# A quantised feed-forward layer as one instruction block over 512-token blocks, its preparation inside the attention ahead of it, whose weights are requested earlier

## The reference

```python
# third attention (z = layernorm(x), c = context, per sequence)
Sim = (z @ w1)[:, None] + (c @ w2)[None, :] + (z * w3) @ c.T + b
A = softmax(Sim, axis=1);  hq = A @ c
Batt = softmax(Sim.max(axis=1));  zbar = Batt @ z
out = concat(z, hq, z * hq, z * zbar) @ W_qv + b_qv

# third feed-forward: fake-quantised
def act_quant(x, clip):     # one scale for the whole tensor
    s = sigmoid(clip) * max(abs(x)) / 127
    return clip(round(x / s), -128, 127) * s
def weight_quant(w):        # one scale per row
    s = max(abs(w), axis=1) / 127
    return clip(round(w / s), -128, 127) * s
xq = act_quant(layernorm(x), clip_x)            # 2048 x 256
gate, up = xq @ weight_quant(w_gate).T, xq @ weight_quant(w_up).T    # 2048 x 704
h = act_quant(silu(gate) * up, clip_down)
x = x + tanh(g) * (h @ weight_quant(w_down).T)
```

## Time and profile before

| | us |
|---|---|
| median of 3 runs (lowest, highest) | 1708.45 (1704.81, 1709.36) |
| the profiled execution, its own time | 1710.01 |
| its span in the profile | 1708.2 |
| third attention, from its first instruction to the layernorm's | 1267.2 to 1374.5 |
| third feed-forward, to the fourth attention's first instruction | 1374.5 to 1497.1 |

### The profile page before, as it was taken

How to read it: one execution, slowest core, us unless ns; L and a number is a source line. 1 busy time by engine, 2 the same in 40 slices (tenths; PEclk the granted TensorE clock), 3 DMA queues, 4 the chain that set the end, 5 groups by cost and what they waited for, 6 DMA issues and landing times. The chain is left out here.

```text
span 1708.2 us, 31848 instructions
## 1 busy us (share of the span) xinstructions
PE 1391.2 (81%) x10246; PEld 1184.1 (69%) x10246; DVE 1155.5 (68%) x2511; ACT 934.1 (55%) x2046; POOL 756.7 (44%) x797
## 2 busy tenths in 40 slices
PE   2599978999999999879973889999758916463898
PEld 0345565999999999745563889999757803253787
DVE  6457654787888878469965478778543458777554
ACT  4246642777777777457731367777326236364332
POOL 2323102466666676513221078888203910235444
PEclk8799987999999999889995989999889958685999
DMA  4000015356656565130023056667310010011001
GB/s 162 12 1 2 1 42 194 139 196 218 225 197 242 188 232 209 60 105 1 2 87 123 2 168 219 212 226 213 112 35 1 1 54 1 1 32 58 0 13 38
DMA packets 62369, 171.87 MB, mean 101 GB/s; under 512 B 11761, under 2 KB 43249, under 8 KB 53057
## 3 DMA queue, kind: packets, MB, share of 16 engines
q1 hardware_dynamic: 53440, 146.50, 24.8%
q0 software_dynamic: 8832, 24.13, 4.5%
HBM read 152.25 MB, written 18.35 MB: 100 GB/s over the span
## 5 line engine op out<-in xcount | busy, mean ns | idle before, releaser
L1706 POOL TENSOR_TENSOR l0m_e_DL<-l0m_e_DN,l0m_e_DH 128x256 fp32r<-128x256 f32 x184 | 182.0, 995 | 121.2 <-ACT l0m_e_DH L1545 74.6
L1489 PE MATMUL PS<-l0m_e_CH,l0m_e_UH 128*128 128x256 f32 x736 | 210.8, 286 | 2.0 <-DVE l0m_e_CL L1639 2.0
L1489 PE MATMUL PS<-l0m_e_CL,l0m_e_UH 128*128 128x256 f32 x736 | 209.0, 284 | 0.0
L1489 PE MATMUL PS<-l0m_e_CH,l0m_e_UL 128*128 128x256 f32 x736 | 208.9, 284 | 0.0
L1611 DVE TENSOR_TENSOR l0m_e_UL<-l0m_e_U,l0m_e_UH 128x512 fp32r<-128x512 f32 x184 | 148.9, 810 | 12.1 <-ACT l0m_e_UH L1536 12.1
L1489 PEld LDWEIGHTS PS<-l0m_e_CH,l0m_e_UH 128*128 128x128 f32 x736 | 141.9, 193 | 2.2 <-ACT l0m_e_UH L1536 2.2
L1489 PEld LDWEIGHTS PS<-l0m_e_CL,l0m_e_UH 128*128 128x128 f32 x736 | 142.0, 193 | 0.0
L1489 PEld LDWEIGHTS PS<-l0m_e_CH,l0m_e_UL 128*128 128x128 f32 x736 | 142.0, 193 | 0.0
L1623 DVE SCALAR_TENSOR_TENSOR Z<-PS,l0m_e_BU,Z 128x256 f32<-128x256 f32 x184 | 88.7, 482 | 73.3 <-ACT Z L1553 70.9
L1553 ACT ACTIVATE Z<-PS,l0m_e_BU 128x256 f32<-128x256 f32 x184 | 87.7, 476 | 83.1 <-PE PS L1489 83.0
L1536 ACT CAST l0m_e_UH<-l0m_e_U 128x512 fp32r<-128x512 f32 x184 | 113.1, 615 | 0.0
(11 more groups left out here) (531 smaller groups left out, 4519.6 us busy)
## 6 DMA issues: line engine op xcount, KB each, us to landing
l0m_e_U<-in_l_up SPq DMA_DIRECT2D x23, 2048.0 KB
...
```

Of the source, the lines that this page charges most:

```text
L1489: ins = nc.tensor.matmul(hb(f)[:, a * SLOTS:(a + 1) * SLOTS], w[:, f % RING, k, a, :], x[:, j, k, :], start=(p == 0), stop=(p == len(passe ...
L1706: nc.gpsimd.tensor_tensor(DL[:, f % RING, :], DN[:, j, f, :], DH[:, f % RING, :].bitcast(F32), ALU.subtract).then_inc(s_dl, 1)
```

## The change

Three things. The third attention's weights are requested by SP in the second layer's last block, in the middle of `Combine.load`, and layers 2 (feed-forward) and 3 (attention) share one `end_layer`, as do the third feed-forward and the fourth attention. Weight preparation, layernorm and the scale of Z are written into the attention's steps. And the feed-forward is one block.

```diff
+        def l2_load(sp):
+            for tile, array in ((l2["WQ"][:, :, :], I["L2_xattn_W_qv"].rearrange("(k p) n -> p k n", p=P)),
+                                (l2["WC"][:, :, :], I["l2_wsim_cols"]), ...
                 for b in range(B):                      # Combine.load
+                    if b == self.RING:
+                        l2_load(sp)
 # l2_attention, sync: l2_bqv_rows, then the feed-forward's clips, up rows and down rows
 # tensor, between queries(t - 4) and out_rows(t - LAG):
+                            if B + 2 <= t < B + 9:
+                                turn_weights(t - B - 2)      # 6 bf16 transposes; the last: one 128x256 f32 product
 # gpsimd, ahead of the steps, and behind them:
+                        nc.gpsimd.partition_all_reduce(f2["SX"][:, 2:3], f2["ONES"][:, 0:1], P, ...)
                         for t in range(B + GROUP + 4):
 ...
+                        pool.wait_ge(f2["s_largest"], 6)
+                        nc.gpsimd.partition_all_reduce(f2["SX"][:, 2:3], f2["PM"][:, 5:6], P, ...)
 # scalar: exp of the clips at t == 4; copies of the turned weights at t = 18 to 24;
 # deviations at t = 19, 23; normalised rows 0 to 3 and 4 to 7 at t = 20, 21, 8 to 11 at t = 24
 # vector, at the end of each step:
+                        def prepare(t):
+                            if t in (2, 3):        # WR: 128 x 6 x 256, to 128 x 6
+                                wch.step(nc.vector.tensor_reduce(WS[:, 1, halves[t - 2]], WR[:, halves[t - 2], :], ...))
+                            if t == 4:             # WD 128 x 2 x 704, then scale and reciprocal
+                            if 5 <= t < 9:         # three a step
+                                for n in range(3 * (t - 5), 3 * (t - 5) + 3):
+                                    wch.step(nc.vector.tensor_scalar(WR[:, n, :], WR[:, n, :], WS[:, 1, n:n + 1], ROUND, ...))
+                            if t == 9:             # two of 128 x 704
+                            if t in (10, 11, 12):  # clip: 128 x 1536, 1536, 1408
+                            if t in (13, 14, 15):  # to bf16: the same sizes
+                            if t == 16:            # DG
+                            prepare(t)
+                            if t == B + 2: next_scales(0)       # statistics of sequences 0 to 7
+                            if t == B + 3: next_factors(0)
+                            if t == B + 6: next_scales(1)       # 8 to 11
+                            if t == B + 7: next_factors(1)
+                            if t in (B + 6, B + 7):             # largest of Z, four sequences each
+                                next_largest(n, 4 * n, 4 * n + 4)
+                        next_scales(2)                          # behind the last step: 12 to 15
+                        next_largest(2, 8, 12)
+                        next_factors(2)
+                        for b in (12, 13): ...                  # normalised rows on DVE (14, 15 on ACT)
+                        next_largest(3, 12, 14)
+                        next_largest(4, 14, 16)
+                        nc.vector.tensor_reduce(PM[:, 5:6], PM[:, 0:5], AX, ALU.max)
+                        dve.wait_ge(f2["s_all_largest"], 2)
+                        scale_steps(wch, SX, CL[:, 0:1])
 # l2_ffn, scalar, one block:
+                        for u, (n, ch) in enumerate(units):
+                            if ch == 0 and 1 <= n and n + 1 < NBLK:
+                                round_z(n + 1)
+                            silu(u)
+                            if ch == 1 and n + 1 < NBLK:
+                                whole_z(n + 1)
+                            if ch == 4 and n + 1 < NBLK:
+                                copy_z(n + 1)
+                        act.wait_ge(s_hst, 2)
+                        for n in range(NBLK):
+                            for q in range(4):
+                                nc.scalar.activation(part, part, ACT.Identity, scale=SH[...], bias=RND[...])   # round, in place
+                                if n >= 1 and q in ACT_PIECES:       # pieces 1 and 2
+                                    whole_h(n - 1, q)
 # l2_ffn, vector:
+                        for u, (n, ch) in enumerate(units):
+                            if ch == 1 and 1 <= n and n + 1 < NBLK:
+                                clip_z(n + 1)
+                            hidden(u)
+                            if u >= 1:
+                                largest(u - 1)
+                        ...
+                        for n in range(NBLK):
+                            for q in range(4):
+                                clip_h(n, q)
+                                if q not in ACT_PIECES:
+                                    whole_h_dve(n, q)
+                                if n >= 1:
+                                    scaled(BT * (n - 1) + q)
+                                    if BT * (n - 1) + q >= 2:
+                                        x_stats(BT * (n - 1) + q - 2)
-        layers = (... (l1_moe,), (l2_attention,), (l2_ffn,), (l3_attention,), (l3_ffn,))
+        layers = (... (l1_moe, l2_attention), (l2_ffn, ahead.close, l3_attention), (l3_ffn,))
```

555 lines of the change are left out of this document (328 added, 227 removed).

## The result

The changed kernel takes 1663.33 us (median of 4 runs, 1655.67 to 1665.76), the kernel before on the same chip 1706.63 (4 runs): ratio 0.974, 95% interval 0.9717 to 0.9763, or 43.3 us less. The prediction said 1664. That the two agree to 0.7 us is in part luck: the stretches that the change touches gave 41.4 us of the 44.8 forecast.

The account below looks back on a forecast made before the run. TensorE bounds the attention's body, GpSimd close behind; between attention and first unit no engine is full. Terms sum to -44.8 us, 1710.01 profiled becoming 1665.2; the median, 1.6 lower, gives 1664, range 1657 to 1673 (chance 0.72).

Parts of the forecast that it names:

- Early request, -7.6: Attention's start: WQ, issued in the block before, lets TensorE's first products start at the block's start, -7.6 us.
- Layer ends, -1.6: Two layer ends become block ends, each costing 0.33 us instead of 1.15: -1.6 us.
- Preparation +2.3: Attention's steps: VectorE's weight preparation, about 17.5 us of work, is mostly hidden and adds 2.3 us, bounds 0 and +14.
- turning +1.7: Attention steps 18 to 24: seven weight transposes on TensorE add 0.85 us ahead of the last context mean, 0.8 behind.
- the 1.0 for holds: Attention's steps: VectorE's weight instructions held by GpSimd's additions make VectorE sometimes later than TensorE's step allows, 1.0 us.
- -41.7 to the first hidden product: Last attention statistics to first hidden product: 55.6 us before, 13.9 after, so -41.7 us.
- the change of code: GpSimd's code load ahead of the scale's reduction: hidden by 1 us; rival, not hidden, 5 to 6 us back, chance 0.08.
- Units +3.3: Feed-forward units: VectorE's clips of Z +1.2, ScalarE's waits and late silu +1.5, cold TensorE +0.6: +3.3 us.
- H and the down product -0.8: H's rounding to the last statistics, pipelined by blocks: 35.2 us before, 34.4 after, bounds 27 and 39.
- the last product and its statistics 4.6: End of H's stage: the final part, behind blocks 2 and 3, takes 4.6 us.
- GpSimd and VectorE holding each other up: Rival, chance 0.12: attention 10 to 18 us longer instead of 4, last stage 2 to 4 more, 1673 to 1681 us.
- starved: Rival of slower or no change, chance 0.02: attention's weight instructions held 4.1 us each by GpSimd, eating 45 us.

Follow-up runs that it names:

- prepare_behind: Changed kernel with weight preparation, turning and copies moved behind the attention's last step: ratio 0.9825 to the kernel before; attention 98.4 us, way to first hidden product 35.4.
- three_edits: Changed kernel with Silu's table loaded early, Z's blocks 2 and 3 converted one unit later, H's block 0 converted directly behind its rounding: ratio 0.9703 to the kernel before.
- two_edits: Changed kernel with Silu's table loaded early and H's block 0 converted directly behind its rounding, Z's conversions unmoved: ratio 0.9752 to the kernel before; units 33.9 us.
- addition_one_column: Changed kernel with GpSimd's sixteen additions to X in the feed-forward's last stage done on one column of 256: H's stage 33.0 us, one run.
- weights_one_element: Changed kernel with VectorE's weight instructions of attention steps 5 to 15 done on one element a row: ratio 0.975 to the kernel before; H's stage 35.1 us.

## Why the prediction was right, point by point

The mechanisms were the forecast ones; several sizes were not, and their errors partly cancel. The attention is the clearest case of luck: 102.6 us forecast, 102.6 measured, by terms that are each 0.6 or 0.7 us too large.

- **Early request, -7.6**: right as a mechanism and in its size. TensorE's first product starts with the block; undoing it costs 7.7 us. Against the profile of the kernel before only 7.0 are left by step 1, as TensorE's clock rose earlier there. The prediction had no term for that.
- **Layer ends, -1.6**: right, -1.1 and -0.8 measured.
- **Preparation +2.3 and turning +1.7**: 4.0 said, 3.3 measured by prepare_behind; with the 7.0 above that makes the -3.6. The preparation costs about 1.3 us where 2.3 stood, the turning 1.1 to 1.4 where 1.7 stood, and the 0.6 to 0.9 left of the 3.3 stay open. Where it shows is as forecast, in the steps with three weight rows (0.6 us by step 8, 0.7 said). The picture behind the 1.0 for holds was wrong in its sizes: I expected VectorE's instructions of 0.95 us to last 1.5 to 2.4 where GpSimd adds. They lasted 0.88 to 1.46, and GpSimd, which I expected to go free, was held for 4.5 us over sixteen instructions, 2.9 of them swallowed by its wait for HC.
- **-41.7 to the first hidden product**: mechanism right, size off by 2.4 us (16.3 us, 13.9 said). Terms that were mis-sized: unit 0 up to its product 4.1 for 3.0, by the table load of 1.28 that I had not listed (three_edits: 1.28 less without it); the layer's end, 1.8 for 1.1; the rest 0.6. That the change of code is hidden is shown: GpSimd waits for the operand, and exposing it costs 5.9. It has 2.2 us to spare, 1 said.
- **Units +3.3**: +2.7. Two clips are 1.4 us of VectorE. ScalarE's two waits for them are there (3.0 us), and VectorE is idle 1.1 us behind them, not 1.5. The cold TensorE that I gave 0.6 cost nothing, because the table load, which I had not counted, gave TensorE that time: in two_edits, without the load, the units are 0.9 longer.
- **H and the down product -0.8**: wrong by 2.1 us, +1.3 measured. The 14.8 us to the end of the first block (14.9) and the holds (3 said, 3.2 to 3.5 measured by addition_one_column) were right. The step that failed is "the last product and its statistics 4.6": it took 6.8, as TensorE ran the first two sequences of the last block and part of the third at the low clock (1.50 us a sequence, 0.87 at the high one), behind 1.8 us of idle time. That is 1.5 of the 2.2 us: the same block at the high clock takes 3.53 for 5.03, and the stage 35.1 for 36.5 (weights_one_element). The other 0.7 us were counted too low without the clock. The prediction had the low clock for the first four sequences alone.

Timeline of that last block:

```profile
1436.53 5.03 PE L2767 MATMUL PS<-l2f_DNT,l2f_HQ 128*128 128x256 bf16 x24 [1.80 <-DVE l2f_HQ L2864]
...
1442.85 0.43 DVE L135 BATCH_NORM_STATS2 STATS<-X 128x6 f32<-128x256 f32 x1 [0.17 <-POOL X L2831]
...
1443.60 0.38 DVE L2131 BATCH_NORM_AGGREGATE MV<-STATS 128x2 f32<-128x6 f32 x4 [0.32 <-PEq L2730]
```

So the sum of the changed stretches is -41.4, not -44.8. The medians differ by 43.3, which leaves 1.9 us for what the change does not touch, within what four runs tell (the changed kernel's four lie 10 us apart). These 1.9 us are what brings the median close to 1664, and nothing in the prediction says where they come from. The rivals: GpSimd and VectorE holding each other up exists, in both directions, at a price of at most 1.3 us in the attention (all that the preparation costs up to step 17) and 3.5 in the last stage, where the rival had 10 to 18 and 2 to 4. The code change was hidden. VectorE's clips and conversions of the weights were never starved, none lasted over 1.46 us.
